# A grid cell of both image halves in one eight-tile stage, with two orders changed around it

## What is computed

```
x = x + L0(groupnorm(x))     # 4x4 grid of 3x3 convolutions
x = x + L1(groupnorm(x))     # one 3x3 convolution, last row and column masked
x = x + L2(groupnorm(x))     # gates from token sums
x = x + L3(groupnorm(x))     # 4x4 grid of 3x3 convolutions, other weights
```

## Time and profile before

| | |
|---|---|
| median of 3 runs | 434.03 us |
| the profiled execution's own time | 435.94 us |
| its span, first to last instruction | 434.1 us, 12447 instructions |
| mean granted TensorE clock | 0.98 of full |
| TensorE matmul busy | 403.1 us of the span |
| VectorE, ScalarE, GpSimd busy | 301.6, 199.4, 205.2 us |

### The profile page before, as it was taken

The page is one execution under the profiler, slowest core; times in us unless marked ns, Lnnn a source line. Parts: engine busy times, 40 slices in busy tenths (PEclk is TensorE's granted clock), DMA queues, the critical chain, the costliest instruction groups (busy, mean ns, idle before and its releaser), DMA issues.

```text
span 434.1 us, 12447 instructions
## 1 busy us (share of the span) xinstructions
PE 403.1 (93%) x5149; PEld 202.5 (47%) x5149; DVE 301.6 (69%) x563; ACT 199.4 (46%) x307; POOL 205.2 (47%) x384
## 2 busy tenths in 40 slices
PE   8999998989999897985998899999999999997884
PEld 5444444445554444543444455445444554444442
DVE  5789967537975346679587789968645954539684
ACT  7555533545526336465201455533545325347363
POOL 6277657955647433300000267657965594442300
PEclk9999999999999998999798999999999999998999
DMA  6076587868879665520000066588677797551701
GB/s 230 13 248 139 130 189 200 190 129 191 186 148 172 130 143 95 122 43 2 1 2 2 12 175 144 127 201 194 155 152 153 142 182 138 98 98 39 111 2 50
DMA packets 27304, 52.90 MB, mean 122 GB/s; under 512 B 11632, under 2 KB 13296, under 8 KB 27248
## 3 DMA queue, kind: packets, MB, share of 16 engines
q1 hardware_dynamic: 14416, 30.24, 30.8%
q0 software_dynamic: 12544, 21.14, 23.4%
q10 hardware_dynamic: 288, 0.72, 0.4%
HBM read 12.81 MB, written 0.52 MB: 31 GB/s over the span
## 4 chain that ended last, share of the span: by engine, by line
PE 57%; POOL 14%; DMA 11%; DVE 8%; ACT 5%; issue 3%; SPq 0%; DVEq 0%; ACTq 0%
PE bank L554 38%; PE bank L598 18%; POOL inp L534 11%; DMA inp<-cell_out 10%; POOL shifts L524 3%; ACT act_out L787 2%; DVE cell_out L1006 2%; DVE inp L718 1%; DVE inp L973 1%; DMA raw<-weights_in 1%; ACT cell_out L781 1%; ACT inp L718 1%; DVE inp L725 1%; DVE stat L860 1%; PE bank L617 1%
## 5 line engine op out<-in xcount | busy, mean ns | idle before, releaser
L534 POOL DMA_DIRECT2D inp<-cell_out x320 | 169.0, 536 | 142.1 <-DVE cell_out L1006 139.1
L787 ACT ACTIVATE act_out<-bank,bias 128x512 f32<-128x512 f32 x160 | 105.3, 687 | 101.3 <-PE bank L598 58.0
L554 PE MATMUL bank<-inp,w_heavy 128*32 128x512 f16 (+1 forms) x1536 | 139.8, 384 | 4.9 <-DMA inp<-cell_out 2.5
L1006 DVE TENSOR_TENSOR cell_out<-act_out,cell_out 128x512 f16<-128x512 f32 x156 | 107.8, 695 | 51.0 <-ACT act_out L787 47.0
L554 PE MATMUL bank<-inp,w_light 96*32 96x512 f16 (+2 forms) x1440 | 119.4, 395 | 12.8 <-DVE inp L973 10.3
L554 PEld LDWEIGHTS bank<-inp,w_heavy 128*32 128x32 f16 (+1 forms) x1536 | 65.1, 102 | 71.0 <-issue 13.8
L554 PEld LDWEIGHTS bank<-inp,w_light 96*32 96x32 f16 (+2 forms) x1440 | 59.8, 104 | 70.7 <-issue 19.8
L781 ACT ACTIVATE cell_out<-bank,bias 128x512 f16<-128x512 f32 x56 | 38.9, 694 | 87.0 <-PE bank L554 64.6
L598 PE MATMUL bank<-cell_out,w_first 32*128 32x512 f16 x1296 | 72.1, 378 | 0.0
L524 POOL DMA_DIRECT2D shifts<-inp x48 | 29.6, 623 | 59.0 <-DMA inp<-cell_out 58.8
L1000 DVE CAST cell_out<-act_out 128x512 f16<-128x512 f32 x100 | 42.9, 429 | 14.2 <-ACT act_out L787 13.5
(11 more groups left out here) (53 smaller groups left out, 170.1 us busy)
## 6 DMA issues: line engine op xcount, KB each, us to landing
inp<-cell_out SPq DMA_DIRECT2D x96, 72.2 KB, 3.6
inp<-cell_out SPq DMA_DIRECT2D x96, 71.2 KB, 3.8
raw<-weights_in SPq DMA_DIRECT2D x8, 672.0 KB, 5.0
inp<-cell_out POOLq DMA_DIRECT2D x128, 36.1 KB, 3.0
raw<-weights_in SPq DMA_DIRECT2D x8, 576.0 KB, 5.0
inp<-cell_out POOLq DMA_DIRECT2D x128, 35.1 KB, 3.2
shifts<-inp POOLq DMA_DIRECT2D x16, 144.5 KB, 3.1
inp<-cell_out POOLq DMA_DIRECT2D x32, 72.2 KB, 4.4
```

What stands on the lines that cost most here:

```text
L534: pool.dma_start(to, source).then_inc(signal, 16)
L554: last = pe.matmul(bank[j % BANKS][p:p + m, :], home[i][0:rows, w:w + m], source[:, off:off + PAIRS, dx:dx + SIDE], start=n == 0, stop=n = ...
L787: act.activation(act_out[:, n % T_RING, :], bank[j % BANKS][:, :], ACT.Relu, bias=bias[:, col + part[k]:col + part[k] + 1], scale=1.0 / W_ ...
L1006: dve.tensor_tensor(low, t, high, ALU.subtract).then_inc(cell_written, 1)
```

## The change

1. Cell (0,3) of both halves becomes one stage. `("cell", 4, 0)` has no banks any more; its two packs stay. In `("cell", 4, 1)` every step has eight matmuls of 32 rows x 64 columns: image t of half b writes partitions 64b to 64b+63 of bank t. Its weights are half as wide, and the four banks hold both halves. Its `up` and `right` leave as 8 DMAs each, two images at a time, where they were 16 of one image each; all come from `cell_out` of the second half.
2. SyncE: at the second half of (0,2) and of (1,2), `up` is put off until after the DMAs of the next stage (the first half of (1,0), or of (2,0)), whose `down` so goes ahead.
3. The pack of the first half of (2,3) moves from behind the only bank of (3,0)'s first half, and the column copies of it, to ahead of that bank's evacuation.

```diff
+def joint(s):
+    return s[0] != "L1" and s[1:] == (0, ROWS - 1)
 def width_of(s):
+    if joint(s):
+        return set_shape(s)[1] * Q
     return 4 * Q if scheme_of(s) == IN_PLACE else set_shape(s)[1] * Q
...
-def lanes_of(c, r, stream):
+def lanes_of(c, r, stream, b):
     outs = streams_out(c, r)
+    if (c, r) == (0, ROWS - 1):
+        return [(t, 2, 2 * Q * b + Q * item_of(r, stream), t) for t in (0, 2)]
...
 def jobs_of(st):
-    return len(jobs_in(*SETS[st[1]][1:])) if st[0] == "cell" else 1
+    if st[0] != "cell":
+        return 1
+    return 0 if joint(SETS[st[1]]) and st[2] == 0 else len(jobs_in(*SETS[st[1]][1:]))
...
-            bank_no = len(jobs[at]) + 1 if m == n - 1 else 0 if soon else 1
+            bank_no = len(jobs[at]) + 1 if m == n - 1 else 0 if soon or ((c, r) == (2, 3) and st[2] == 0) else 1
...
+            def put_off(st):
+                return st[2] == 1 and (SETS[st[1]][1:] == (0, 2) or SETS[st[1]][1:] == (1, 2))
+            def sent_at(at):
+                found = [(cells[at], [True] if put_off(cells[at]) else [True, False])]
+                if at and put_off(cells[at - 1]):
+                    found.append((cells[at - 1], [False]))
+                return found
...
-                for k, signal, source, to in moves(st):
-                    if k > bank_no:
-                        sp.wait_ge(cell_written, emptied[jobs[st][k]][1])
-                    bank_no = k
-                    sp.dma_start(to, source).then_inc(signal, 16)
-                if bank_no < len(jobs[st]) - 1:
+                for o, wanted in sent_at(at):
+                    bank_no = -1
+                    for k, signal, source, to in moves(o):
+                        if (signal.name in down_names) not in wanted:
+                            continue
+                        if k > bank_no:
+                            sp.wait_ge(cell_written, emptied[jobs[o][k]][1])
+                        bank_no = k
+                        sp.dma_start(to, source).then_inc(signal, 16)
+                if jobs[st]:
                     sp.wait_ge(cell_written, written(st))
...
-                        last = pe.matmul(bank[jobs[st][t] % BANKS][:, :],
-                                         home[i][lanes, block_no * 4 * Q:block_no * 4 * Q + 4 * Q],
-                                         source[lanes, first:first + PAIRS, dx:dx + SIDE],
+                        m = 2 * Q if both else 4 * Q
+                        for part, source in enumerate(sources):
+                            last = pe.matmul(bank[jobs[st][t] % BANKS][m * part:m * part + m, :],
+                                             home[i][lanes, block_no * m:block_no * m + m],
+                                             source[lanes, first:first + PAIRS, dx:dx + SIDE],
...
+                if not jobs[st]:
+                    for bank_no in range(2):
+                        pack(st, bank_no)
+                    return
```

More of the change, by code:

```diff
@@ L338, in moves @@
                 tc, tr = target(c, r, s)
-                if tc == COLS or tc == 0 or (queue == "pool") != (s == RIGHT):
+                if not jobs[st] or tc == COLS or tc == 0 or (queue == "pool") != (s == RIGHT) or s in copied(c, r):
                     continue
[L341 to L345, removed]
+                quad = places(tc, tr, s)[0][1]
+                for b in range(HALVES) if joint(SETS[i]) else [h]:
+                    goal = inp[b][tr].rearrange("p i e a x -> p i e (a x)")
+                    for image, each, lane, slot in lanes_of(c, r, s, b):
                         for par in range(2):
@@ L349, in moves @@
                             length = 2 * each * STORED * PITCH - par * PITCH
[L350 to L354, removed]
+                            give, take = (v.rearrange("p i e x -> p (i e x)") for v in
+                                          (source[p:p + C, slot:slot + each], goal[d:d + C, image:image + each]))
+                            found.append((slot + each - 1, arrival(b, tr, s), give[:, 0:length],
+                                          take[:, par * PITCH:par * PITCH + length]))
             return sorted(found, key=lambda move: move[0])
@@ L367, in copies @@
                 quad = places(tc, tr, s)[0][1]
-                for t, (image, each, p, slot) in enumerate(lanes_of(c, r, s)):
+                for t, (image, each, p, slot) in enumerate(lanes_of(c, r, s, b)):
                     if COPIED_BY[t] != engine:
@@ L433, in build @@
                 tc, tr = target(c, r, s)
-                signal = arrival(b, tr, s) if tc < COLS else None
-                n = len([m for m in moves(st) + moves(st, "pool") if m[1] is signal])
-                if n:
+                for signal in [arrival(h, tr, s) for h in range(HALVES)] if tc < COLS else []:
+                    n = len([m for m in moves(st) + moves(st, "pool") if m[1] is signal])
+                    if not n:
+                        continue
                     totals[signal.name] = totals.get(signal.name, 0) + 16 * n
@@ L465, in _ @@
         def _(sp):
+            down_names = [moved[b, r, DOWN].name for b in range(HALVES) for r in range(ROWS)]
+            def put_off(st):
[5 more added lines that the diff above has]
+                return found
             def load_weights(p):
@@ L566, in conv_in_place @@
                 entered = (i, b) in entries
-                above = None if entered else next(o for o in halves[b] if SETS[o[1]] == (SETS[i][0], 0, r - 1))
+                both = joint(SETS[i])
+                above = [next(o for o in halves[h] if SETS[o[1]] == (SETS[i][0], 0, r - 1))
+                         for h in (range(HALVES) if both else [b])] if not entered else []
                 steps = products(IN_PLACE)
@@ L1110, in in_place_set @@
                         if 0 <= ky < 3:
-                            v[t, p_in, :, off, :, (t + n) % NI, p_out, :] = part[:, :, ky, :].transpose(1, 2, 0)
-    return v.reshape(4 * Q, NINE * 4 * Q)
+                            v[t, p_in, :, off, :, (t + n) % NI if slots == NI else n, p_out, :] = part[:, :, ky, :].transpose(1, 2, 0)
+    return v.reshape(4 * Q, NINE * slots * Q)
 def weight_set(w, outs, how):
```

36 lines of the change are left out of this document (20 added, 16 removed).

## The result

The changed kernel takes **453.81 us** (median; 453.18 to 456.55), the kernel before 434.01 us in the same comparison: a ratio of 1.0468, with a 95% interval of 1.0425 to 1.0511. The forecast was 435.6 us, in a range up to 440. The sign was right; the size, 1.6 us, was wrong by a factor of twelve.

A forecast was written before the change was run, and what follows sets the result against it. Bound: (1,1) starts when `down` of (1,0) lands, with (0,3)'s matmuls as cover. First layer 0 - 1.2 + 0.5, last 1.8 + 0.5: 1.6 us more, 435.6 us; 8-in-10 range 430.5 to 440.

The forecast's parts named there:

- (0,3) is cover, not time: At (0,3): its matmuls only cover `down` of (1,0) travelling; the joint stage takes 6.04 us, and that saving is worth nothing.
- (1,1)'s start: At (1,1): `down` of (1,0) issued as before, landing 2.0 us (first layer) and 1.8 us (last) sooner; TensorE idles 5.4 and 4.1.
- Up to (1,2): From (1,1) to (1,2): SyncE, VectorE and DMA chain starts (1,2) unchanged in the first layer, 1.8 us later in the last.
- the landing: In the chain to (1,2): a DMA takes 2.9 us to land, up to 4.1 beside other load.
- Part 2's gain at (2,1) and (2,2): At (2,1) and (2,2): earlier `down` and weight load cut waits by 1.2 us in the first layer, 0 in the last.
- Part 3: At (2,3): the moved pack shifts the idle time by one half; +0.5 us in each layer.
- The clock: Behind the idle time ahead of (1,1): a lower granted clock costs 1.7 us in each layer.
- the clock stays up: Rival: no clock loss; hidden at (1,1), 1.4 us twice at (2,3), giving 432.8 us; chance 0.10.
- the put-off `up` crowds more: Rival: other transfers make each landing 1 us longer, 4 us a layer on the chain, giving 440 us; chance 0.08.
- The transfers keep ahead: Rival: four landings before `down` of (1,1) take 2.1 us, so (1,2) starts sooner; 432.4 or 429.6 us; chance 0.22.

The follow-up runs named there:

- e17: The changed kernel with two weight loads moved behind `down` of (1,1)'s first half: 449.73 us, 1.0367 of the kernel before.
- e12: The kernel before with `up` put off at (0,2) alone and a weight load moved behind the 16 `up` of (0,3): 445.63 us, ratio 1.0309.
- e15: The kernel before with `up` put off at (0,2) alone and two weight loads moved behind `down` of (1,1)'s first half: 440.14 us, ratio 1.0162.
- e10: The kernel before with `up` put off at (0,2) alone: 447.54 us, ratio 1.0328.
- e11: The kernel before with `up` put off at (1,2) alone: 433.40 us, ratio 0.9989.
- e4: The kernel before with only the pack of (2,3)'s first half moved: 435.90 us, ratio 1.0028.
- e7: The changed kernel with idle TensorE work ahead of (1,1) and (1,2) in both layers: 453.64 us, 1.0453 of the kernel before.
- e8: The kernel before with idle TensorE work of 22 matmuls ahead of (2,3)'s first half in both layers: 432.10 us, ratio 0.9984.

## Why the prediction was right or wrong

- **(0,3) is cover, not time** (step 1): right. The joint piece took 6.17 and 6.16 us (forecast 6.04), and no version with it beat the kernel before. The Trainium skill's page "TensorEngine Tiling (Array Packing)", section "Tiling Modes", lists eight independent tiles of this size, and the trace agrees.
- **(1,1)'s start**: `down` of (1,0) was issued at 59.02, 56.8 with the start-up taken off, as forecast. The waits were 3.73 and 5.68 us (forecast 5.4 and 4.1), the starts 3.5 and 0.2 us earlier than before, not 2.0 and 1.8. It did not matter, since (1,2) set the time.
- **Up to (1,2)**: this is the step that failed. It said "no change" for the first layer and 1.8 us for the last; 5.0 and 7.0 came out. The chain was the right one, link by link; the mis-sized term is the landing, 2.9 us in the forecast. With 2.2 us of start-up added to the forecast's times, in the first layer: the last put-off `up` was issued on time, at 67.66 (forecast 67.4), and landed at 73.5, not 70.3. VectorE made up some of that, and the joint `up` went at 77.80, not 75.7. Its sixth DMA, the last that the pack for (1,2) needs, landed at 87.4, not 82.1. Both took 5.9 us. The link behind them was priced well: `down` of (1,1) landed 3.7 us after its issue, for 4.1. In the last layer the put-off `up` landed in 2.0 us; there `down` of (1,0)'s second half was late (with 8.0 us added its landing was forecast for 306.8, and VectorE's pack for it began at 309.84), and the joint `up`'s sixth DMA took 5.5 us.
- Why the joint `up` lands so late is known in part. The 2.9 us came from the earlier trace rows, and those DMAs carry one image; the joint stage's carry two. SyncE's issues in that stretch of the kernel before (73 to 80 us), and those of the changed kernel (77.5 to 83.5), with the median landing:

```profile
inp<-cell_out SPq DMA_DIRECT2D x5, 35.1 KB, 2.9
...
inp<-cell_out SPq DMA_DIRECT2D x4, 71.2 KB, 5.0
```

  A weight load is not needed for it: in e17, with none near, that sixth DMA took 6.3 us. But size isn't shown to be the whole either, since the 36 KB DMAs of e12 took 4.7 us; no run separates size from what GpSimd sends beside it. The prediction had 4.8 to 7.2 us at hand in the earlier trace rows and used it only for `down` of (1,0).
- What the step left out altogether is the two weight loads. It followed every stream that is moved past SyncE's queue, and not the 672 KB load of 63.68 that the moved streams push to a worse moment, nor the one behind it. With the put-off alone the two are about half of its cost or more (e15 against e10); in the changed kernel moving them gives back 1.0 of 4.7 points, and 2.6 once the packs are out of the way.
- **Part 2's gain at (2,1) and (2,2)**: (2,1)'s 0.73 us did vanish, (2,2)'s fell from 1.19 to 0.65: 1.3 us, forecast 1.2. But alone (e11) it can't be told from nothing.
- **Part 3**: +0.5 a layer forecast; the second half waits 3.05 and 2.78 us, with a granted clock of 0.71 behind the first of these, and e4 gives 1.0028, 1.2 us for both layers with an interval that holds 0. From (2,0) to the end of the last layer the changed kernel is 0.7 us longer. Right, so far as it can be seen.
- **The clock**: 1.7 us a layer at (1,1) was forecast, hidden in the first. Low clocks of 0.57 and 0.60 were there, and e7 shows them hidden. At (1,2) the sum has no clock term, since it saw no long wait coming there; the waits of 8.59 and 4.29 us brought one, with clocks of 0.50 and 0.51 behind them, and 2.0 and 1.6 us were paid: 3.6 of the 15.1 us, the second term missing from the sum. The Trainium skill's page "TensorE: Matmul & The Clock Gate", Part 1, says an idle TensorE falls to 1.2 GHz; the trace agrees (0.50 behind (1,2)'s wait of 8.59 us). The price is paid where the next start waits for nothing else, as at (2,0), and hidden where it does, as at (1,2). For the same reason the 1.4 us a layer that the rival "the clock stays up" takes at (2,3) was too much: e8's profile shows 0.8 and 0.6.
- **The rivals**: "the put-off `up` crowds more" came nearest, with a chance of 0.08. It took 1 us more per landing, where the two that mattered took 3.0 more each in the first layer, and its sum was too small even so: 4 us in each of two layers is 443.6, not 440. "The transfers keep ahead" (0.22) had more, on the argument of fewer and larger DMAs; e17 shows these landing in 5.0 us (median) with no load near, so fewer and larger bought nothing. The right sign rests on the last layer's 1.8 us at (1,2), the same chain that came out longer, so it was not luck alone; but slower had a chance of 0.50 only, and 453.8 lies far outside the range up to 440.

## What to carry to other kernels

When DMAs are put off, place everything that shares their queue on the new time line, weight loads included, and ask for each what it will now stand ahead of; then take landing times from DMAs of the same size in a stretch with the same traffic, not from smaller ones in a quiet one. A late start can cost twice, by the wait and by the slow clock behind it. An in-order engine that waits for a transfer with evacuations queued behind it turns one late landing into a chain of them, so before a producer is made faster or a transfer later, move the waits behind the work that doesn't need them. And when taking away one suspected cause gives little, look at whether the next one has taken its place before dropping it: here 2.0 and 1.0 points apart were 4.6 together.

## What was not expected of the hardware

- Eight matmuls of 32x64 run together fully: 216 in 6.17 us are 28.6 ns each, where 216 of 32x128 in 12.08 us are 55.9 ns.
- The landing of one and the same stream depends on its company by a factor of 2.4: `down` of (1,1) landed in 2.6 us (e15), and in 6.3 us behind two weight loads (e12); `up` of (0,3) in 4.7 us (e12) and in 7.2 us right behind one (e10).
